# One-hot lists of tokens in BF16, and batch attention's constants made in the recurrent block

## What is computed

```python
x = _layernorm(x + attention(x))             # 16 heads, relative positions, causal
x = _layernorm(x + experts(x, 14, top 2) + two shared experts(x))
x = _layernorm(x + rwkv(x))                  # a recurrent scan over 256 positions
x = _layernorm(x + batch_attention(x) + experts(x, 8, top 2))   # attention over the 32 batches
```

## Time and profile before

| | |
|---|---|
| median of 3 runs | 2475.6 us (2472.62 to 2476.64) |
| the profiled execution's own time | 2475.63 us |
| its span in the profile | 2473.9 us |
| `choose_experts` of moe0 | 846 to 930 us |
| `route` of moe0 | 930 to about 1210 us |
| `recur` | about 1215 to 1559 us |
| `attend_batches` | 1559 to 1908 us |
| `choose_experts` of moe1 | 1962 to 2022 us |
| `route` of moe1 | 2023 to 2470 us |

### The profile page before, as it was taken

How to read it: one execution, slowest core, us unless ns; L and a number is a source line. 1 busy time by engine, 2 the same in 40 slices (tenths; PEclk the granted TensorE clock), 3 DMA queues, 4 the chain that set the end, 5 groups by cost and what they waited for, 6 DMA issues and landing times. The chain is left out here.

```text
span 2473.9 us, 52699 instructions
## 1 busy us (share of the span) xinstructions
PE 1946.5 (79%) x16756; PEld 1600.7 (65%) x16788; DVE 1531.0 (62%) x6215; ACT 1275.3 (52%) x3105; POOL 1046.7 (42%) x1285
## 2 busy tenths in 40 slices
PE   7799999999997897999578888599998758856610
PEld 6455555555555886877467777488887757755500
DVE  2478788888886583421279997588887564313345
ACT  3588888888884322333258887344443104423310
POOL 2133333333331315555478885222222115566654
PEclk9799999999998898999889999799999559977655
DMA  7799999999995104555412221000001115533323
GB/s 237 254 313 311 312 311 317 313 311 312 312 313 164 56 1 124 154 154 151 108 29 58 60 60 44 18 1 2 1 1 30 74 34 155 155 114 110 101 73 74
DMA packets 198092, 353.95 MB, mean 143 GB/s; under 512 B 25280, under 2 KB 145856, under 8 KB 196800
## 3 DMA queue, kind: packets, MB, share of 16 engines
q1 hardware_dynamic: 140752, 294.77, 36.6%
q0 software_dynamic: 17664, 36.21, 6.2%
q10 hardware_dynamic: 39408, 19.60, 2.7%
HBM read 165.87 MB, written 145.52 MB: 126 GB/s over the span
## 5 line engine op out<-in xcount | busy, mean ns | idle before, releaser
L1389 POOL DMA_INDIRECT moe_route_rows_sb<-tokens,moe_taken x296 | 279.8, 945 | 291.7 <-PE moe_route_bank L1429 145.6
L177 POOL TENSOR_SCALAR_AFFINE_SELECT heads_raw_relative<-heads_raw_relative 128x508 f32<-128x508 f32 x256 | 166.7, 675 | 500.8 <-ACT heads_raw_relative L562 460.9
L1547 DVE COPY moe_route_y<-moe_route_bank 128x128 f32<-128x128 f32 x296 | 86.1, 291 | 427.3 <-PE moe_route_bank L1448 218.9
L1488 ACT COPY moe_route_rows_t<-moe_route_bank 128x128 f32<-128x128 f32 x296 | 78.4, 265 | 435.0 <-PE moe_route_bank L1429 270.1
L1438 PE MATMUL moe_route_bank<-moe_route_rows_t,moe_route_w_now 128*128 128x128 f32 x1184 | 220.9, 315 | 85.7 <-issue 74.9
L562 ACT COPY heads_raw_relative<-heads_rel_bank 128x768 f32<-128x768 f32 x247 | 198.7, 804 | 125.6 <-PE heads_rel_bank L457 125.5
L1448 PE MATMUL moe_route_bank<-moe_w,moe_route_hid 128*128 x1184 | 218.9, 312 | 47.3 <-issue 24.8
L486 PE MATMUL attend_turn_bank<-ident,attend_score 128*128 128x128 f32 x1536 | 232.0, 287 | 20.5 <-ACT attend_prob_t L568 19.2
L1438 PEld LDWEIGHTS moe_route_bank<-moe_route_rows_t,moe_route_w_now 128*128 128x128 f32 x1184 | 180.3, 217 | 103.8 <-issue 98.9
L486 PEld LDWEIGHTS attend_turn_bank<-ident,attend_score 128*128 128x128 f32 x1536 | 163.8, 142 | 117.5 <-ACT attend_prob_t L568 68.1
L568 ACT ACTIVATE attend_prob_t<-attend_turn_bank 128x384 f32<-128x384 f32 x512 | 224.8, 500 | 6.9 <-PE attend_turn_bank L486 6.9
(11 more groups left out here) (321 smaller groups left out, 5072.4 us busy)
## 6 DMA issues: line engine op xcount, KB each, us to landing
shear<-heads_raw_relative SPq DMA_DIRECT2D x128, 768.0 KB, 5.5
heads_relative<-shear SPq DMA_DIRECT2D x128, 768.0 KB, 6.4
moe_route_w_now<-moe_w SPq DMA_DIRECT2D x296, 129.0 KB
expert_out<-moe_route_y ACTq DMA_DIRECT2D x73, 256.0 KB
qk_heads<-project_qk SPq DMA_DIRECT2D x32, 256.0 KB, 4.3
heads_qk<-qk_heads SPq DMA_DIRECT2D x128, 64.0 KB
tokens<-moe_z SPq DMA_DIRECT2D x8, 1024.0 KB, 4.1
moe_route_rows_sb<-tokens,moe_taken POOLq DMA_INDIRECT x296
```

The costliest lines, as they stand in the source:

```text
L177: m = nc.gpsimd.affine_select(out=future, in_=future, compare_op=ALU.is_ge, fill=-BIG, base=1 - P, pattern=[[0, QUAD], [1, P - 1]], channe ...
L1389: nc.gpsimd.indirect_dma_start(rows_sb[:, s % TAKEN, :], None, c.tokens, bass.IndirectOffsetOnAxis(ex.taken[:, s // S, s % S:s % S + 1], 0 ...
```

## The change

**Lists.** `at_low` and `at_token` become BF16 tensors of their own and no longer lie in `ex.z`. A token's number (up to 8191) has more bits than BF16 keeps, so two smaller numbers go in its place: `at_token` has two halves of `even_steps` columns (78 for moe0, 72 for moe1), one with the partition's number and one with the column's number, and the list is 64 x the first product + the second. In a part of `choose_experts` `at_low` is now made by eight `tensor_scalar` in place of one `tensor_tensor`, `at_token` by sixteen in place of eight; PE has one BF16 matmul of 156 or 144 columns per column of choices in place of a float32 one of 77 or 71. In `route` there are three DVE instructions per listed column in place of two. `taken` is made by a copy out of PSUM and a multiply-add in place of a copy.

**Constants.** A class `BatchConstants` holds them outside of both blocks. Its loads are issued in `recur` on SP behind the store of the first tile, its masks are made by POOL at the end of `recur`.

```diff
@@ choose_experts, DVE
             dve.wait_ge(made, 8)
             nc.vector.tensor_copy(low_no[:, :], low_i[:, :])
-            nc.vector.tensor_copy(step_no[:, :], step_i[:, :])
-            nc.vector.tensor_copy(token_no[:, :], token_i[:, :, :].rearrange("p t k -> p (t k)"))
+            nc.vector.memset(step_no[:, :, :], -1.0).then_inc(blank, 1)
+            dve.wait_ge(blank, 1)
+            nc.vector.tensor_copy(step_no[:, :, 0:S], step_i[:, :].rearrange("p (g s) -> p g s", g=GROUPS))
+            nc.vector.tensor_copy(ex.row_no[:, :], row_i[:, :])
+            nc.vector.tensor_copy(ex.column_no[:, :], column_i[:, :])
...
-            dve.wait_ge(c.tokens_out[ex.name], 16 * 4)
             for part in range(half // PART):
-                r, cols = part % 2, slice(part * COLS, (part + 1) * COLS)
+                r = part % 2
                 wait_past(dve, inverted, part - 1)
-                nc.vector.tensor_tensor(at_low[r][:, :, :], along(low_no[:, :], COLS), bcast(low[:, cols], P), ALU.is_equal
-                                        ).then_inc(lows_done, 1)
                 for k in range(COLS):
                     col = part * COLS + k
-                    s = nc.vector.tensor_scalar(at_token[r][:, k, :], step_no[:, 0:S], high[:, col:col + 1], token_no[:, col:col + 1],
-                                                ALU.is_equal, ALU.mult)
+                    s = nc.vector.tensor_scalar(at_low[r][:, k, :], low_no[:, :], low[:, col:col + 1], None, ALU.is_equal)
+                s.then_inc(lows_done, 1)
+                for k in range(COLS):
+                    col = part * COLS + k
+                    for v, number in enumerate((ex.row_no[:, 0:1], ex.column_no[:, col // TOPK:col // TOPK + 1])):
+                        s = nc.vector.tensor_scalar(at_token[r][:, k, v, :], step_no[:, 0, :], high[:, col:col + 1], number,
+                                                    ALU.is_equal, ALU.mult)
                 s.then_inc(valued, 1)
...
-            nc.vector.tensor_copy(ex.taken[:, 0, :], token_bank[:, 0:S])
+            nc.vector.tensor_copy(part_list[:, :], token_bank[:, EVEN:EVEN + S]).then_inc(listed, 1)
+            dve.wait_ge(listed, 1)
+            nc.vector.scalar_tensor_tensor(out=ex.taken[:, 0, :], in0=token_bank[:, 0:S], scalar=float(NT), in1=part_list[:, :],
+                                           op0=ALU.mult, op1=ALU.add)
@@ recur, SP
                 if t:
                     regroup(t - 1)
+                if t == 0:
+                    fixed.load(sp, a)
@@ recur, POOL, behind the loop of turns
+            fixed.masks(pool)
```

More of the change, by code:

```diff
@@ L1099, in choose_experts @@
         PART = 4
-        COLS, S = PART * TOPK, ex.group_steps
-        low_i, step_i, token_i = sb("low_int", [P, P], I32), sb("step_int", [P, GROUPS * S], I32), sb("token_int", [P, NT, TOPK], I32)
-        low_no, step_no, token_no, high, low = ex.low_no, ex.step_no, ex.token_no, ex.high, ex.low
+        COLS, S, EVEN = PART * TOPK, ex.group_steps, ex.even_steps
+        low_i, step_i = sb("low_int", [P, P], I32), sb("step_int", [P, GROUPS * S], I32)
+        row_i, column_i = sb("row_int", [P, 1], I32), sb("column_int", [P, NT], I32)
+        low_no, step_no, high, low = ex.low_no, ex.step_no, ex.high, ex.low
+        part_list = sb("part_list", [P, S])
         high_i = sb("high_int", [P, NT * TOPK], I32)
-        at_low, at_token = ([ex.z[:, (2 * w + u) * COLS:(2 * w + u + 1) * COLS, 0:size] for u in range(2)]
-                            for w, size in enumerate((P, S)))
-        lows_done, valued, inverted = sem("lows_done"), sem("valued"), sem("inverted")
+        at_low = [sb(f"at_low{u}", [P, COLS, P], BF16) for u in range(2)]
+        at_token = [sb(f"at_token{u}", [P, COLS, 2, EVEN], BF16) for u in range(2)]
+        lows_done, valued, inverted, listed, blank = (sem(x) for x in ("lows_done", "valued", "inverted", "listed", "blank"))
         rank_bank, tile_bank = ([psum(f"{x}{u}") for u in range(2)] for x in ("rank_bank", "tile_bank"))
@@ L1337, in route @@
         sb, psum, sem = scope(nc, ctx, f"{ex.name}_route")
-        at_low, at_token = ([sb(f"{x}{u}", [P, w]) for u in range(2)] for x, w in (("at_low", P), ("at_token", S)))
-        valued, inverse_made, listed = sem("valued"), sem("inverse_made"), sem("listed")
+        EVEN = ex.even_steps
+        at_low, at_token = ([sb(f"{x}{u}", [P, w], BF16) for u in range(2)] for x, w in (("at_low", P), ("at_token", 2 * EVEN)))
+        part_list = sb("part_list", [P, S])
+        valued, inverse_made, part_kept, listed = sem("valued"), sem("inverse_made"), sem("part_kept"), sem("listed")
         rows_sb, y = sb("rows_sb", [P, TAKEN, D]), sb("y", [P, 2, CH, D])
@@ L1452, in list_tokens @@
                 pe.wait_ge(valued, k + 1)
-                nc.tensor.matmul(token_bank[:, 0:S], at_low[k % 2][:, :], at_token[k % 2][:, :], start=k == 0, stop=k == LISTED - 1
+                nc.tensor.matmul(token_bank[:, 0:2 * EVEN], at_low[k % 2][:, :], at_token[k % 2][:, :], start=k == 0, stop=k == LISTED - 1
                                  ).then_inc(inverse_made, 1)
@@ L1625, in _ @@
                     dve.wait_ge(inverse_made, LISTED)
-                    nc.vector.tensor_copy(ex.taken[:, 1, :], token_bank[:, 0:S]).then_inc(listed, 1)
+                    nc.vector.tensor_copy(part_list[:, :], token_bank[:, EVEN:EVEN + S]).then_inc(part_kept, 1)
+                    dve.wait_ge(part_kept, 1)
+                    nc.vector.scalar_tensor_tensor(out=ex.taken[:, 1, :], in0=token_bank[:, 0:S], scalar=float(NT),
+                                                   in1=part_list[:, :], op0=ALU.mult, op1=ALU.add).then_inc(listed, 1)
                 if s in late and late[s][1] == "output":
@@ L1648, in recur @@
+def recur(nc, c, choice, groups, fixed):
     a = c.a
@@ L2178, in attend_batches @@
         block = ctx.enter_context(nc.Block())
[L2179 to L2188 removed]
+        loads = fixed.LOADS
@@ L2201, in _ @@
-            work = of_head[:, :, :]
-            nc.gpsimd.memset(work, 1.0).then_inc(made, 1)
-            pool.wait_ge(made, 4)
-            nc.gpsimd.affine_select(out=work, in_=work, compare_op=ALU.is_ge, fill=0.0, base=0,
-                                    pattern=[[-HB * HD, HB], [-HD, HB]], channel_multiplier=1).then_inc(made, 1)
-            pool.wait_ge(made, 5)
-            nc.gpsimd.affine_select(out=work, in_=work, compare_op=ALU.is_ge, fill=0.0, base=HD - 1,
-                                    pattern=[[HB * HD, HB], [HD, HB]], channel_multiplier=-1).then_inc(made, 1)
@@ L2219, in _ @@
-            nc.gpsimd.memset(causal_f[:, :], 0.0).then_inc(made, 1)
-            pool.wait_ge(made, 10)
-            for b in range(HB):
-                s = nc.gpsimd.affine_select(out=causal_f[b * B:(b + 1) * B, :], in_=causal_f[b * B:(b + 1) * B, :],
-                                            compare_op=ALU.is_ge, fill=-BIG, base=0, pattern=[[0, NPG * HB], [-1, B]],
-                                            channel_multiplier=1)
-            s.then_inc(made, 1)
             def normalise_probs(g, u):
@@ L2530, in build @@
         groups = ctx.enter_context(nc.sbuf_tensor("groups", [P, NT, D + 1], F32))
-        recur(nc, c, choice0, groups)
-        attend_batches(nc, c, groups)
+        fixed = BatchConstants(nc, ctx)
+        recur(nc, c, choice0, groups, fixed)
+        attend_batches(nc, c, groups, fixed)
         with ExitStack() as second:
```

116 lines of the change are left out of this document (70 added, 46 removed).

## The result

The changed kernel takes 2489.09 us (median of 5 runs, 2487.82 to 2495.4), the one before 2476.64 us beside it (5 runs, 2472.62 to 2479.45): ratio 1.0064, 95% interval 1.0049 to 1.0079. It is slower by 12.5 us by the medians and by 15.9 us by the ratio (12.1 to 19.3); forecast were 2489.0 us, +13.5 us, and slower with a chance of 0.75. Every ratio here leaves out three executions that took far longer than the others of their kernel: 2657.18 and 2949.86 us of the kernel before, 4589.78 us of e5.

The account below looks back on a forecast made before the run. DVE was taken to set the lists' length, POOL's masks the start of `attend_batches`. 8.5 + 10.4 + 0.5 + 0.9 - 1.8 - 5.5 + 0.5 = +13.5 us on 2475.63 us: 2489 us, range 2471 to 2501 us.

Parts of the forecast that it names:

- The price of DVE's small instructions: In `choose_experts`' lists: 0.13 us with one per-partition operand, 0.19 with two, plus columns; a part 4.7 us against 2.98.
- moe1's list: In moe1's `choose_experts`: eight parts take 37.4 us in place of 27.0, +10.4 us.
- moe0's: In moe0's `choose_experts`: the list takes 37.4 + 1.8 us in place of 30.7, +8.5 us.
- The POOL additions: In moe0's list: four POOL additions fall beside a DVE that no longer waits, 0.45 us each, 1.8 us.
- The constants: At the start of `attend_batches`: constants stand ready at 1559.37 us, `row_bias` waits 0.3 us for PE, -5.5 us.
- Heads and tails: Around the lists: +0.25 us at each head, twice; `taken`'s second instruction +0.3 us in both `choose_experts`.
- The extra clearing block: At the kernel's end: one more block with barriers and a clear costs about +0.5 us.
- moe1's second `taken`: In moe1's `route`: a second instruction for `taken` behind a wait, for which POOL stands, +0.3 us.
- `route`'s -1.8 us: In both `route`s: the shorter listing saves 1.8 us, somewhat under half of at most 5 us.
- PE at the low clock: Rival in moe0's list: PE at half speed, two parts 10.8 us against DVE's 9.8, +4 us, 2493 us; chance 15%.
- the first rival: In the lists: BF16 small instructions cost about 0.1 us, a part 2.4 us, each list -8, 2454 us; chance 13%.
- let go late; I see no cause: Rival in `route`: shorter listing breaks the pattern of late steps, 1.4 us a step, -34 us, 2455 us; chance 3%.

Follow-up runs that it names:

- e5: The changed kernel with a part's one-hot rows in `choose_experts` made together, 7 DVE instructions in place of 24: 2337.47 us, ratio 0.9935.
- e3: The changed kernel with the column's number as an immediate in `choose_experts`, for half of the `at_token` instructions: 2358.54 us, ratio 1.0021.
- e10: The changed kernel with `at_low` made on 64 of its 128 columns only in `choose_experts`: one execution, 2481.17 us.
- e7: The changed kernel with batch attention's six loads issued at the start of `attend_batches` again, the masks staying in `recur`: one run, 2485.31 us.
- e8: The changed kernel with POOL's masks made at the start of `attend_batches` again, the six loads staying in `recur`: one run, 2491.01 us.
- e2: The changed kernel with the batch constants left in `attend_batches`, so only the lists change: 2370.89 us, ratio 1.0079.
- e6: The changed kernel with `route`'s listing in float32 again, two DVE instructions per column and `taken` as one copy: 2483.27 us, ratio 1.004.
- e1: The kernel before with only the batch constants (loads and masks) moved into `recur`, the lists as before: 2346.49 us, ratio 0.9973.
- e9: The same kernel as e5 (changed kernel, 7 DVE instructions a part in place of 24), run again: 2460.77 us, ratio 0.9925.
- e4: The changed kernel with a part's eight `at_low` made by one `tensor_tensor` on 128 x 1024 in `choose_experts`: 2483.91 us, ratio 1.0041.

## Why the prediction was right

- **The price of DVE's small instructions** was right: 0.13 and 0.19 us without columns, BF16 columns at half of the float32 price, 4.7 us a part; measured 4.68 and 4.64 us. e3 shows the second operand's share, e10 the column's. What had been only chosen, the middle between "columns cost nothing" and "as in float32", is measured now: 0.00025 us.
- **moe1's list** +10.07 us (forecast +10.4), **moe0's** +8.68 us (+8.5). Subtracting whole stretches took DVE's old 5.6 us of waiting in correctly. The POOL additions cost little more than was set (four at 0.45 us, 1.8 us): the four parts that they hit are longer than 4.68 us by 0.51, 0.43, 0.51 and 0.56 us, 2.0 us in all. The two lists differ by 2.35 us; the 6 more columns are 0.2 of the rest (128 x 6 x 0.00025).
- **The constants**: -5.6 us (forecast -5.5); the cover was SP's last read, as named. To let all engines stand for POOL's chain of masks was too narrow a reading: in the earlier trace rows PE is let go by the loads only 1.1 us before DVE by the masks, and e7 and e8 show that the two are worth something only together. DMA was also not nearly idle in `recur` (a share of 0.25 from 1300 to 1400 us in the kernel before), yet the stage did not grow (333.3 and 333.04 us).
- **Heads and tails**: +0.56 and +0.1 us at the heads (0.25 each), -0.23 and +0.28 us at the tails (0.3 each). In moe0's tail 0.41 us came back beside it: before, a POOL addition (922.05 us) fell on L1295, which was 0.61 us long; now that addition falls in the list, and the same instruction (L1304) is 0.20 us long.
- **The extra clearing block**: from the end of SP's last store row to the end of the span it is 4.36 us in the kernel before and in e2, the two without this block, and 4.64 to 4.77 us in the nine other profiles: +0.3 to +0.4 us (forecast +0.5). The 0.3 us for moe1's second `taken` is not seen alone.
- **The term that failed** is `route`'s -1.8 us. I took the 0.04 us between steps with and without a listing for a price of which some part could be had; e6, and e1 beside e2 and e3, show no gain. Without this term the sum would be +15.3 us, and the measurement (12.5 by medians, 15.9 by the ratio) does not tell the two sums apart. The heads, lists, tails, constants and clearing block alone came to +14.2 us, where +15.0 had been forecast for them; that +13.5 lies as near as it does to 12.5 is in part luck.
- **PE at the low clock** came true as a state and not as a price. Three of the eight groups of eight passes took 1.20 us, at a granted clock of 0.50 (1.2 GHz), and PE had waited 4.58, 3.48 and 4.48 us before them; the other five took 0.71 us, at a granted clock of 1.00 (2.4 GHz) (PE's timeline, below). DVE never waited for PE, so the time was DVE's anyway.
- **The rule of the skill** (the Trainium skill, "VectorE: DVE Perf Modes", section "The TRN2 errata": 58 cycles and the columns over the speed-up) would have given about the 2454 us of the first rival. Its slope holds here: e10's 0.00025 us per column is a quarter of a cycle at its 0.96 GHz. Its fixed part doesn't: 0.13 us with one operand and 0.19 us with two, where 58 cycles are 0.06. The same section adds that the row is too low for a single copy that was measured, whose fixed part was about 150 cycles; that is 0.16 us, between the two prices found here. The same section's advice, that a large tile pays the fixed part once and many small ones each time, agrees with e9: its two lists are 29.3 us shorter than the changed kernel's (39.75 + 37.40 - 26.19 - 21.70).

```profile
895.56 1.20 PE L1172 MATMUL moe_choose_tile_bank<-moe_choose_at_token,moe_choose_at_low 128*128 128x156 bf16 x8 [4.58 <-DVE moe_choose_at_token L1299]
900.23 1.20 PE L1172 MATMUL moe_choose_tile_bank<-moe_choose_at_token,moe_choose_at_low 128*128 128x156 bf16 x8 [3.48 <-DVE moe_choose_at_token L1299]
901.22 3.65 PE L839 MATMUL moe_choose_shared_bank<-shared_zt,shared_w 128*128 128x256 f32 x8
...
906.50 0.71 PE L1172 MATMUL moe_choose_tile_bank<-moe_choose_at_token,moe_choose_at_low 128*128 128x156 bf16 x8
```

## What to carry to other kernels

Before small matrices are changed to a faster type for the matmul's sake, count the instructions that make them and price each by the distance of starts of its nearest kin in the trace, operands first and columns last: here PE had 5.6 us to give and DVE took 24 instructions a part for it. Where several things are waited for together, the trace names only the last; ask what each is worth alone, because moving one of two may gain nothing.

## What the runs showed of the hardware that was not expected

**A `tensor_tensor` with a float32 broadcast operand gains nothing from BF16 in its other input and its output**: 1.14 us for 128 x 1024 either way; with 0.67 us for 576 columns in e9 that is 0.0010 us per column, where `tensor_scalar` pays a quarter of that per BF16 column. The Trainium skill, "VectorE: DVE Perf Modes", section "The perf-mode tier table (the rule you actually need)", gives `tensor_tensor` twice the speed in BF16. No run here tests that: `low` and `high` are float32 in all of them, and whether the float32 type or the broadcast holds this form back is open.

**The same kernel was 5% faster beside e1, e2, e3 and e5, nearly all of it in `route`.** The kernel before took 2353 us there and 2472 us beside e4, on the same chip. It left no trace at 2353 us, so e1's is used. From moe0's `choose_experts` on, e1's stages equal those of before within 0.7 us (but for the constants), while the two `route`s take 249.58 and 363.22 us in place of 283.2 and 450.42: 121 us of the 136 us between the two profiled executions. Another 7.9 us lie ahead of moe0's `choose_experts` (846.2 and 838.3 us), a stretch that was as short in e7 (836.8 us), at the longer time; the constants are the 5.6 us. The windows of moe1's and moe0's `route` (us; busy and count of PE, PEld, DVE, ACT, POOL; PE's clock, DMA share, GB/s), in the kernel before:

```profile
2023.48:2473.90 450.42, 230.10 (x1406) 208.20 (x1406) 161.15 (x629) 125.06 (x442) 256.00 (x270) 0.73 0.40 112
931.00:1214.20 283.20, 247.50 (x1802) 223.12 (x1802) 77.68 (x293) 98.72 (x332) 145.55 (x155) 0.96 0.51 144
```

and in e1:

```profile
1974.98:2338.20 363.22, 215.12 (x1406) 190.90 (x1406) 161.79 (x629) 125.59 (x442) 255.85 (x270) 0.76 0.50 139
923.22:1172.80 249.58, 239.56 (x1802) 219.00 (x1802) 78.71 (x293) 98.87 (x332) 145.77 (x155) 0.98 0.58 164
```

The same instructions and DVE, ACT and POOL times, PE's busy time only 15 and 8 us less, but more GB/s. ACT's waits in moe1's `route` of the kernel before name the transfer (us in total, times, longest), a wait that e1 has not at all:

```profile
ACT moe_route_rows_t L1488 <- DMA moe_route_w_now<-moe_w: 101.6, 26, 7.5
```

So I read that the experts' weights, when they come late, set the pace of moe1's `route`: that is what I had called steps "let go late; I see no cause" in the prediction. It is read from the traces, not tried, and in the changed kernel the trace names no instruction for the like wait (98.9 us). Why the same transfers went faster there is open, and no run tried it.
